# Building the turned one-hots of graph attention on ScalarE instead of VectorE

## The chip, the cores and the metric

The kernel is one program on one core of a Trainium2 chip. The metric is the device time of one execution in microseconds (us), taken as the median of several runs. TensorE is called PE in the profile, VectorE DVE, ScalarE ACT, GpSimd POOL and SyncE SP.

## The reference, cut to what matters

Four graph layers run over 6250 nodes (7 tiles of 128 rows at a time, 49 tiles in all) and 206,250 edges that are sorted by destination. The change lies in the third of the four, a graph attention with three inner layers and four heads:

```python
def _gat_layer(x, src, dst, W_i, a_src_i, a_dst_i, b_i):
    h = (x @ W_i).reshape(n, H, C)
    es = einsum('nhc,hc->nh', h, a_src_i)
    ed = einsum('nhc,hc->nh', h, a_dst_i)
    e = es[src] + ed[dst]                       # a score for each edge and head
    e = where(e > 0, e, 0.2 * e)
    m = segment_max(e, dst); p = exp(e - m[dst])
    denom = segment_sum(p, dst)
    out = segment_sum((p / denom[dst])[:, :, None] * h[src], dst)
```

The lookup `ed[dst]` is done as a matrix product: for 128 edges at a time a matrix with nodes on partitions and edges along the row, one where the node is the edge's destination and zero elsewhere, is multiplied with the nodes' scores. That matrix is the "turned one-hot", `pick_t`. The plain one-hot `pick` (edges on partitions) sums the weighted rows by destination.

## The kernel before, in words

The edges are cut into slots of 128, and 32 slots make a group. An attention layer has 52 groups, so the three layers have 156. Each group goes through these steps, and neighbouring groups overlap:

- **Gather (POOL, L649).** 32 indirect DMAs, one for each slot, fetch the rows of the source nodes from `row_table` into one of two halves of `gathered`. Before each round of 8 POOL waits for `att.summed`: the sums of the group that used this half two groups earlier. POOL does nothing else in an attention layer. In all there are 4992 of these gathers.
- **Destination scores.** SP loads the destinations of the group's edges, the same for all partitions, into `pick_t` (L508, 128 x 4096 bf16, 1 MB). Two instructions (L1769, `build_pick_t`) turn this in place into one-hots by comparing each number with the partition's own index. PE multiplies them with `dst_parts` (L1110, `score_some`).
- **Scores, maxima, exponents (DVE with PE and ACT).** `score_edges` waits for the landing of the whole group's gathers and ends in L1782 and L1785; `first_scans` (L1792, L1794), `carries` (L1799 to L1807), `last_scans` (L1813 to L1824) and `shift_scores` (L1829 to L1834) find the maximum of each destination. ACT takes the exponents (L829, L831).
- **Weighing and summing.** For each batch of 4 slots DVE weighs the gathered rows (`weigh`, L1853), PE multiplies them with `pick` (`sum_batch`, L1182), and DVE adds the results to `acc` (`add_batch`, L1866).
- **Plain one-hots (ACT).** `act_picks` builds 8 slots of `pick`: 8 instructions at L804 (the distance between a column's number and the edge's destination) and one at L807 (one less the distance, cut at zero).

The order is written out by hand in `dve_group`, `pe_group` and `act_group`. While group g is summed in its eight batches m = 0 to 7, the steps of group g+1 are put between the batches on DVE: scores after m = 0, first scans after 1, carries and the first half of `build_pick_t` (for group g+2) after 2, last scans and the second half of `build_pick_t` after 3, the shift after 5. In the first two layers DVE also scans edge attributes after m = 4 and m = 6 (`scan_edges`, L1535 and L1537), whose results PE turns (L1122) and ACT copies (L755).

ACT goes through a group in this order: `stage` (L824: it waits until the next group's gathers have landed and writes the indices of the group after that), then for each quarter q of the group `act_picks`, which waits until PE has summed the batches of that quarter; between the third and the fourth quarter come `scan_out` and `act_exps`.

The semaphores that tie this together: SP counts up `att.rows_loaded` when a load of `pick_t` has landed; who builds counts up `att.turned` once for each half; PE waits for it in `score_some` and counts up `att.dst_scored`, for which SP waits before the next load.

```python
def build_pick_t(part_no):
    ks = slice(part_no * GROUP // 2, (part_no + 1) * GROUP // 2)
    dve.tensor_scalar(pick_t[:, ks, :], pick_t[:, ks, :], part_index[:, 0:1], None,
                      ALU.is_equal).then_inc(att.turned, 1)
```

## Time and profile before

| what | value |
|---|---|
| median of 3 runs | 9245.97 us (9245.64 to 9248.44) |
| the profiled execution's own time | 9241.63 us |
| its span, first to last instruction | 9239.8 us |
| mean granted TensorE clock | 0.642 of full speed |
| PE busy | 5626.5 us, 61% |
| DVE busy | 5638.8 us, 61% |
| ACT busy | 3271.8 us, 35% |
| POOL busy | 5375.1 us, 58% |
| HBM | 106 GB/s over the span |

"Busy" counts the time in which an engine's instructions run, over the whole span; the stages have different limits, so a share says little by itself. In a row of the costliest groups, the numbers behind the first bar are the busy time in us and the mean duration of one instruction in ns, and those behind the second bar are the idle time of the engine before these instructions and what ended most of it. "issue" means that the engine waited for nothing that the profile shows. In a timeline each row has the start in us, the time in us, the engine, the line of the kernel, the operation, what it writes and reads, and how many instructions it merges; in brackets the idle time before it.

### The profile page before, as it was taken

The page shows a single profiled execution, that of the slowest core. Times are in us where ns is not written, and L with a number is a line of the kernel's source. Part 1 is how long each engine was busy: PE and PEld are TensorE (multiplying, and loading weights), DVE is VectorE, ACT ScalarE, POOL GpSimd, SP SyncE. Part 2 cuts the span into 40 slices and gives each one's busy share as a digit, 9 for nine tenths or more (in the row PEclk, how much of TensorE's full clock was granted, in tenths as well). Part 3 has the DMA queues.
Part 4 walks back from the last instruction along what each step waited for, and adds up shares of the span by engine and source line. Part 5 has one row for each costly group of instructions (what it writes and reads, how often), then busy time and mean ns, then how long its engine had stood idle before and what let it go on. Part 6 is the DMA issues. An engine that isn't in the chain of part 4 may idle for free.

```text
span 9239.8 us, 129442 instructions
## 1 busy us (share of the span) xinstructions
PE 5626.5 (61%) x34288; PEld 4513.0 (49%) x34288; DVE 5638.8 (61%) x13019; ACT 3271.8 (35%) x7522; POOL 5375.1 (58%) x5192
## 2 busy tenths in 40 slices
PE   4999879964555555555455555555534545445456
PEld 3777646653544445444444444454434444444444
DVE  6888721135666666666466666666645555555555
ACT  3555400023333333333343333333323333333334
POOL 2000100047777777775677777777657777777770
PEclk9999989965555555555555555555555555555558
DMA  3333335404444444443344444444423333233321
GB/s 101 136 139 139 125 140 192 175 16 120 119 119 116 122 113 124 114 116 82 96 113 118 119 116 121 113 123 113 104 65 80 85 80 85 79 85 80 85 79 32
DMA packets 601474, 989.07 MB, mean 107 GB/s; under 512 B 331107, under 2 KB 455044, under 8 KB 561524
## 3 DMA queue, kind: packets, MB, share of 16 engines
q0 software_dynamic: 163760, 357.05, 17.1%
q1 hardware_dynamic: 217540, 544.34, 16.8%
q10 hardware_dynamic: 219648, 81.82, 3.4%
q8 instruction: 192, 3.15, 0.1%
q14 instruction: 334, 2.73, 0.1%
HBM read 758.42 MB, written 224.34 MB: 106 GB/s over the span
## 4 chain that ended last, share of the span: by engine, by line
PE 27%; DVE 22%; DVEq 18%; POOL 14%; issue 13%; DMA 5%; ACT 1%; POOLq 0%; SPq 0%; ACTq 0%
DVEq L1264 15%; PE bank L959 13%; POOL arena L649 13%; DVE acc L1866 10%; DMA arena<-row_table,staged_idx 4%; PE bank L1182 3%; PE bank L984 3%; DVE arena L1853 2%; DVE arena L1822 2%; PE bank L1122 2%; DVEq L1866 2%; DVE x_mem L1535 1%; DVE arena L1815 1%; DVEq L1858 1%; PE bank L1247 1%
## 5 line engine op out<-in xcount | busy, mean ns | idle before, releaser
L649 POOL DMA_INDIRECT arena<-row_table,staged_idx x4992 | 5087.9, 1019 | 1626.1 <-issue 1467.3
L1182 PE MATMUL bank<-arena 128*128 128x136 f32 x9984 | 2487.9, 429 | 1207.5 <-DVE acc L1866 1045.8
L1182 PEld LDWEIGHTS bank<-arena 128*128 128x128 f32 x9984 | 2195.9, 316 | 1372.1 <-issue 1231.0
L1866 DVE TENSOR_TENSOR acc<-acc,bank 128x136 f32 x4992 | 1476.7, 296 | 1020.7 <-issue 798.1
L804 ACT ACTIVATE pick_dist<-col,dst_local 128x128 bf16<-128x128 f32 x4992 | 1523.3, 388 | 1092.0 <-PE bank L1182 1091.3
L959 PE MATMUL bank<-arena 128*128 128x385 bf16 (+1 forms) x7546 | 1342.6, 327 | 49.5 <-DVE arena L1639 33.0
L597 POOL TENSOR_TENSOR arena<-acc,node_stat 128x896 f32 x14 | 24.5, 1748 | 1721.8 <-POOLq L609 956.3
L959 PEld LDWEIGHTS bank<-arena 128*128 128x128 bf16 x7546 | 711.2, 98 | 476.5 <-DVE arena L1639 33.2
L1138 PE MATMUL bank<-ident,arena 128*32 128x128 f32 x624 | 161.5, 414 | 1206.8 <-DVE arena L1785 1206.8
L1853 DVE TENSOR_TENSOR arena<-arena,prob 128x528 f32<-128x528 f32 x1248 | 841.6, 695 | 0.2
L1782 DVE TENSOR_TENSOR arena<-arena 128x128 f32<-128x128 f32 x156 | 60.8, 390 | 1229.2 <-DMA arena<-row_table,staged_idx 1229.2
L807 ACT ACTIVATE arena<-pick_dist,ones 128x1024 f32<-128x1024 bf16 x624 | 716.4, 1148 | 45.4 <-issue 3.2
L1508 DVE TENSOR_TENSOR arena<-key_line,x_mem 128x1024 bf16<-128x1024 bf16 x1216 | 690.5, 625 | 65.4 <-PE bank L984 51.6
L1138 PEld LDWEIGHTS bank<-ident,arena 128*32 128x32 f32 x624 | 67.0, 129 | 1258.2 <-DVE arena L1785 1238.6
L745 ACT CAST arena<-bank 128x784 bf16<-128x784 f32 x608 | 507.7, 849 | 409.4 <-PE bank L984 409.4
L1110 PE MATMUL bank<-dst_parts,arena 128*128 x4992 | 480.4, 184 | 160.5 <-issue 107.0
L824 ACT CAST staged_idx<-src_of 128x32 int32<-128x32 f32 x153 | 33.3, 218 | 1529.0 <-DMA arena<-row_table,staged_idx 1529.0
L1110 PEld LDWEIGHTS bank<-dst_parts,arena 128*128 128x128 bf16 x4992 | 390.8, 107 | 249.1 <-issue 190.6
L1122 PE MATMUL bank<-ident,x_mem 96*128 96x96 f32 x1664 | 313.4, 369 | 283.9 <-DVE x_mem L1537 283.9
L1122 PEld LDWEIGHTS bank<-ident,x_mem 96*128 96x128 f32 x1664 | 259.0, 223 | 343.1 <-issue 343.1
L755 ACT COPY x_mem<-bank 128x384 f32<-128x384 f32 x416 | 178.9, 482 | 566.7 <-PE bank L1122 552.2
L984 PE MATMUL bank<-arena 128*128 128x98 bf16 x4864 | 321.9, 210 | 0.0
(354 smaller groups left out, 5383.0 us busy)
## 6 DMA issues: line engine op xcount, KB each, us to landing
arena<-dst_rows SPq DMA_DIRECT2D x156, 1024.0 KB
cell_rows<-arena SPq DMA_DIRECT2D x76, 1568.0 KB, 5.2
arena<-cell_rows SPq DMA_DIRECT2D x76, 1568.0 KB, 6.5
arena<-row_table,staged_idx POOLq DMA_INDIRECT x4992
edge_stats<-x_mem ACTq DMA_DIRECT2D x416, 192.0 KB, 3.5
x_mem<-in_edge_attr SPq DMA_DIRECT2D x208, 192.0 KB
x_mem<-segment_flags SPq DMA_DIRECT2D x416, 96.0 KB
arena<-change_rows SPq DMA_DIRECT2D x312, 64.0 KB
```

The source lines that it names most:

```text
L649: pool.indirect_dma_start(gathered[:, at, :], None, table, bass.IndirectOffsetOnAxis(staged_idx[:, at:at + 1], 0)).then_inc(att_gathered[n ...
L804: nc.scalar.activation(pick_dist[:, k, :], col_index[:, :], ACT.Abs, scale=-1.0, bias=dst_local[:, bass.ds(slot + k, 1)])
L807: nc.scalar.activation(pick[:, where:where + ROUND, :], pick_dist[:, :, :], ACT.Relu, scale=-1.0, bias=ones[:, 0:1]).then_inc(att.picked, 1)
L959: mm = pe.matmul(bank[:, 4 + b, 0:width], cell_mem[f][:, j * P:(j + 1) * P], Hp[:, j, 0:width], start=j == 0, stop=j == NT - 1)
L984: mm = pe.matmul(bank[:, at_bank, at_col:at_col + CELLS], hot_src[:, r // PAIR, :, r % PAIR], hot_cell[:, r // PAIR, :, r % PAIR], start=T ...
L1110: mm = pe.matmul(bank[:, 2, k * PARTS * HEADS:(k + 1) * PARTS * HEADS], pick_t[:, k, :], dst_parts[:, bass.ds(at[k % 4], PARTS * HEADS)], ...
L1122: mm = pe.transpose(bank[:, m, c * 2 * EA:(c + 1) * 2 * EA], scanned[:, c * P:(c + 1) * P], ident[0:2 * EA, 0:2 * EA])
L1182: mm = pe.matmul(region(k)[:, 0:ROW], pick[:, k, :], gathered[:, b * GROUP + k, :], start=True, stop=True)
L1264: dve.drain()
L1508: made = dve.tensor_tensor(hot[:, first:first + UNIT // PAIR, :, :], key_line[:, 0:width * PAIR].rearrange("p (c t) -> p c t", t=PAIR).uns ...
L1853: dve.tensor_tensor(batch_rows, batch_rows, prob[:, b, :, m * BATCH:(m + 1) * BATCH].rearrange("p h s -> p s h").unsqueeze(3) .to_broadcas ...
L1866: done = dve.tensor_tensor(row, row, region(m * BATCH + k), ALU.add)
```

## The change

ScalarE builds `pick_t` in place of VectorE. Where VectorE did it in one instruction for each half (16 slots), ScalarE needs two: the distance of each number from the partition's index (Abs with a bias of minus the index, in place, bf16), then one less the distance, cut at zero (Relu with scale -1 and bias 1, in place). A vector `minus_part` is made for it once, before the layers. In `act_group` the two halves stand behind `act_picks` of the first and of the second quarter. At the start of a layer all four halves (of the first two groups) stand behind the layer's first `act_picks` and before the first `stage`. The waits for `att.rows_loaded` move along. VectorE keeps all else in the same order.

```diff
+        minus_part = sb("minus_part", [P, 1])
...
+            def build_pick_t(rows, part_no):
+                ks = slice(part_no * GROUP // 2, (part_no + 1) * GROUP // 2)
+                if part_no == 0:
+                    act.wait_ge(att.rows_loaded, 16 * rows)
+                    act.sem_inc(act_tick, 1)
+                nc.scalar.activation(pick_t[:, ks, :], pick_t[:, ks, :], ACT.Abs, bias=minus_part[:, 0:1])
+                act.drain()
+                nc.scalar.activation(pick_t[:, ks, :], pick_t[:, ks, :], ACT.Relu, scale=-1.0,
+                                     bias=ones[:, 0:1]).then_inc(att.turned, 1)
...
                             act_picks(q * ROUND, it * (2 * GROUP) + (b + 1) * GROUP + q * ROUND)
+                        if ahead and q < 2:
+                            build_pick_t(n * NG + g + 3, q)
...
+                for part_no in range(2):
+                    build_pick_t(n * NG + 1, part_no)
+                for part_no in range(2):
+                    build_pick_t(n * NG + 2, part_no)
                 stage(0, 0, 0)
...
+            dve.tensor_scalar(minus_part[:, :], part_index[:, :], -1.0, None, ALU.mult)
...
-                def build_pick_t(part_no):
-                    ks = slice(part_no * GROUP // 2, (part_no + 1) * GROUP // 2)
-                    dve.tensor_scalar(pick_t[:, ks, :], pick_t[:, ks, :], part_index[:, 0:1], None,
-                                      ALU.is_equal).then_inc(att.turned, 1)
-
...
-                        if ahead and m == 2:
-                            dve.wait_ge(att.rows_loaded, 16 * (n * NG + 3 + b) + it * 32)
-                            build_pick_t(0)
                         if head and m == 3:
                             last_scans(G + 1, 1 - b)
-                        if ahead and m == 3:
-                            build_pick_t(1)
...
-                dve.wait_ge(att.rows_loaded, 16 * (n * NG + 1))
-                for part_no in range(2):
-                    build_pick_t(part_no)
...
-                dve.wait_ge(att.rows_loaded, 16 * (n * NG + 2))
-                for part_no in range(2):
-                    build_pick_t(part_no)
```

How the order on two engines moves, at the places of which the prediction speaks. First DVE in a group of the first layers, before: the end of `last_scans` (L1819 to L1824), the second half of `build_pick_t` (L1769) and the start of the next weighing.

```order
L1819 TENSOR_TENSOR arena<-arena,cross_rows 32x4
L1822 SCALAR_TENSOR_TENSOR arena<-arena 32x512
L1824 SCALAR_TENSOR_TENSOR arena<-arena 32x512
L1769 TENSOR_SCALAR arena<-arena,part_index 128x2048
L1853 TENSOR_TENSOR arena<-arena,prob 128x4x132
L1858 TENSOR_LOAD offsets
```

The same place with the change, where the lines have other numbers (L1835 and L1837 are the two scans, L1866 is the weighing):

```order
L1832 TENSOR_TENSOR arena<-arena,cross_rows 32x4
L1835 SCALAR_TENSOR_TENSOR arena<-arena 32x512
L1837 SCALAR_TENSOR_TENSOR arena<-arena 32x512
L1866 TENSOR_TENSOR arena<-arena,prob 128x4x132
L1871 TENSOR_LOAD offsets
```

The weighing now follows the second scan directly. The other half of `build_pick_t` goes from behind L1807 in the same way. Then ACT from the start of a group on, before: `stage`, and `act_picks` of three quarters.

```order
L824 CAST staged_idx<-src_of 128x32
L804 ACTIVATE pick_dist<-col,dst_local 128x128 x8
L807 ACTIVATE arena<-pick_dist,ones 128x1024
L804 ACTIVATE pick_dist<-col,dst_local 128x128 x8
L807 ACTIVATE arena<-pick_dist,ones 128x1024
L804 ACTIVATE pick_dist<-col,dst_local 128x128 x8
L807 ACTIVATE arena<-pick_dist,ones 128x1024
```

And with the change (L817 is the distance and L819 the cut, 16 slots each):

```order
L835 CAST staged_idx<-src_of 128x32
L805 ACTIVATE pick_dist<-col,dst_local 128x128 x8
L808 ACTIVATE arena<-pick_dist,ones 128x1024
L817 ACTIVATE arena<-arena,minus_part 128x2048
L819 ACTIVATE arena<-arena,ones 128x2048
L805 ACTIVATE pick_dist<-col,dst_local 128x128 x8
L808 ACTIVATE arena<-pick_dist,ones 128x1024
L817 ACTIVATE arena<-arena,minus_part 128x2048
L819 ACTIVATE arena<-arena,ones 128x2048
L805 ACTIVATE pick_dist<-col,dst_local 128x128 x8
L808 ACTIVATE arena<-pick_dist,ones 128x1024
```

Four instructions of 2048 elements came in between the first and the third quarter; nothing else on ACT changed its place.

## Rows read from the trace of the kernel before

**Rows 1.** The page's costliest groups: POOL's gathers.
```profile
L649 POOL DMA_INDIRECT arena<-row_table,staged_idx x4992 | 5087.9, 1019 | 1626.1 <-issue 1467.3
```

**Rows 2.** L649 alone by layer: ns min/median/max, first and last start in us.
```profile
L649 POOL DMA_INDIRECT arena<-row_table,staged_idx x1664: 940/944/2412, 2079.5 to 4298.0; - x185
...
L649 POOL DMA_INDIRECT arena<-row_table,staged_idx x1664: 940/944/2402, 4450.0 to 6669.3; - x185
...
L649 POOL DMA_INDIRECT arena<-row_table,staged_idx x1664: 938/944/2287, 6856.3 to 9024.5; - x185
```

**Rows 3.** POOL's waits from 2100 to 4290: total us, times, longest us.
```profile
POOL arena L649 <- issue: 480.0, 1574, 0.3
```

**Rows 4.** Timeline of one group of the first layer (4085.03 to 4127.39), rows of DVE and POOL.
```profile
4095.05 0.78 DVE L1769 TENSOR_SCALAR arena<-arena,part_index 128x2048 bf16<-128x2048 bf16 x1
4095.61 1.02 POOL L649 DMA_INDIRECT arena<-row_table,staged_idx  x1 [0.30 <-issue]
4095.75 0.69 DVE L1853 TENSOR_TENSOR arena<-arena,prob 128x528 f32<-128x528 f32 x1
...
4099.51 1.21 DVE L1822 TENSOR_TENSOR_SCAN arena<-arena 32x512 f32<-32x512 f32 x1
4100.69 1.01 POOL L649 DMA_INDIRECT arena<-row_table,staged_idx  x1 [0.30 <-PE bank L1182]
...
4101.94 0.72 DVE L1769 TENSOR_SCALAR arena<-arena,part_index 128x2048 bf16<-128x2048 bf16 x1
4102.01 1.46 POOL L649 DMA_INDIRECT arena<-row_table,staged_idx  x1 [0.30 <-issue]
...
4102.58 0.69 DVE L1853 TENSOR_TENSOR arena<-arena,prob 128x528 f32<-128x528 f32 x1
...
4105.05 1.28 DVE L1535 TENSOR_TENSOR_SCAN x_mem<-x_mem 96x512 f32<-96x512 bf16 x1
...
4107.45 0.68 DVE L1853 TENSOR_TENSOR arena<-arena,prob 128x528 f32<-128x528 f32 x1
4107.52 1.42 POOL L649 DMA_INDIRECT arena<-row_table,staged_idx  x1 [0.30 <-issue]
...
4112.27 1.28 DVE L1535 TENSOR_TENSOR_SCAN x_mem<-x_mem 96x512 f32<-96x512 bf16 x1
4113.00 1.30 POOL L649 DMA_INDIRECT arena<-row_table,staged_idx  x1 [0.30 <-issue]
```

**Rows 5.** Timeline of two other groups nearby, rows of DVE and POOL.
```profile
3970.40 1.21 DVE L1822 TENSOR_TENSOR_SCAN arena<-arena 32x512 f32<-32x512 f32 x1
3970.95 1.64 POOL L649 DMA_INDIRECT arena<-row_table,staged_idx  x1 [0.30 <-issue]
...
3972.83 0.72 DVE L1769 TENSOR_SCALAR arena<-arena,part_index 128x2048 bf16<-128x2048 bf16 x1
3972.90 1.47 POOL L649 DMA_INDIRECT arena<-row_table,staged_idx  x1 [0.30 <-issue]
...
4069.91 1.28 DVE L1535 TENSOR_TENSOR_SCAN x_mem<-x_mem 96x512 f32<-96x512 bf16 x1
4070.01 1.93 POOL L649 DMA_INDIRECT arena<-row_table,staged_idx  x1 [0.30 <-issue]
```

**Rows 6.** Timeline of a third group: its two scans at L1535.
```profile
4019.62 1.28 DVE L1535 TENSOR_TENSOR_SCAN x_mem<-x_mem 96x512 f32<-96x512 bf16 x1
...
4027.21 1.28 DVE L1535 TENSOR_TENSOR_SCAN x_mem<-x_mem 96x512 f32<-96x512 bf16 x1
```

**Rows 7.** L1769 alone: duration, first and last start, and what it waited for.
```profile
L1769 DVE TENSOR_SCALAR arena<-arena,part_index x312: 703/734/797, 2097.3 to 9001.4; 128x2048 bf16<-128x2048 bf16 x156
...
  DMA arena<-dst_rows: 6.9, 1
```

**Rows 8.** The page's costliest groups: ACT's plain one-hots.
```profile
L804 ACT ACTIVATE pick_dist<-col,dst_local 128x128 bf16<-128x128 f32 x4992 | 1523.3, 388 | 1092.0 <-PE bank L1182 1091.3
...
L807 ACT ACTIVATE arena<-pick_dist,ones 128x1024 f32<-128x1024 bf16 x624 | 716.4, 1148 | 45.4 <-issue 3.2
```

## Prediction

> **What bounds the kernel now.** I read the page first: PE and DVE are both busy for 61% of the span, ACT for 35%, POOL for 58%, and no share names a bound. So I took the attention layers apart, since the change lies in them alone. The row of POOL's gathers [rows 1] shows 4992 of them with 5087.9 us busy, and an idle time of which nearly all is "issue". By layer [rows 2] they run from 2079.5 to 4298.0, from 4450.0 to 6669.3 and from 6856.3 to 9024.5, which is 6606 us of the 9240. The question is whether POOL waits for anybody inside a layer. It does not: in the first layer its longest wait of 1574 is 0.3 us [rows 3], the pause that follows every gather. The 0.94 us of a median gather and that pause (1.247 us together) make 39.9 us for a group of 32, but a layer of 52 groups takes 42.7 us for each (2219 us) and the last one 41.7 us (2169 us). What is missing lies inside the gathers: 5087.9 less 4992 times 0.944 is 375 us, in gathers that take up to 2.4 us instead of 0.94 [rows 1, 2]. **The layers are bound by POOL's gathers, and only the length of a gather can move their time.** The chain of waits gives DVE a large share, but POOL never stands still for DVE's results.
>
> What makes a gather long is seen in the timeline [rows 4]. The gather at 4107.52 takes 1.42 us; a weighing (L1853) began 0.07 us before it and ended at 4108.13, 0.61 us into it. The gather at 4113.00 takes 1.30 us; the scan L1535 runs until 4113.55. The gather at 4102.01 takes 1.46 us beside a L1769 that began 0.07 us earlier. Each time the gather ends 0.75 to 0.82 us after the DVE instruction does. So a gather that starts while DVE is inside an instruction with its inputs in SBUF is held until that instruction ends, and one that starts first is not: L1822 at 4099.51 began 0.07 us after its gather, which took the plain 1.25 us to the next one at 4100.69. The scan L1822 holds longest: in another group it began 0.55 us before a gather, which took 1.64 us [rows 5]. What a DVE instruction costs is therefore decided by its place against the gathers, to 0.1 us.
>
> The Trainium skill (page "SBUF — State Buffer", section "Who interferes with whom") says that DVE and GpSimd share one pair of ports, that a tensor_scalar in a two-port mode locks GpSimd out, and that a tensor_tensor with both inputs in SBUF does so only against GpSimd's reads, so not against the writing of descriptors. The trace agrees with the lock and not with the exception: gathers are held behind L1853 and L1535 too [rows 4]. By that rule only L1769 would hold gathers, which is the second rival below.
>
> **The change part by part.**
> *ACT gets four instructions of 2048 elements for each group.* L804 takes 388 ns for 128 elements and L807 takes 1148 ns for 1024 [rows 8], 0.85 ns for each further element, so one of 2048 takes about 2.0 us and a group 8.1 us. Before its L804 ACT idles 1092 us for PE's sums, 7.0 us in each of 156 groups, and the builds stand right there. So about 1 us may run over into the third quarter, whose one-hots are wanted a whole group later. Cost 0; if that cover were gone it would be 8.1 us for each group on ACT, which is busy 35%. PE gets the first half of `pick_t` earlier than before. The load of the destinations must have landed a few us earlier than for DVE; DVE waited for it once in 312 times, at the start of the first layer [rows 7], so it landed well ahead. If it did land late, ACT would stand and POOL would not notice, up to the some 8 us that ACT has left. The bounds of this part are 0 and, were all four instructions to delay POOL, 8.1 us times 156; nothing in the rows points above 0.
>
> *Start of a layer.* ACT builds four halves (16 us) behind the first one-hots, while the first group's 32 gathers need 40 us to land. Hidden; 0.
>
> *DVE loses L1769, 312 times.* It frees 0.70 us at the first place (L1769 at 4095.05, the next weighing at 4095.75) and 0.64 us at the second (4101.94 to 4102.58) [rows 4]. As time on DVE this is worth nothing, because POOL does not wait for DVE. But two things follow for the gathers. L1769 no longer holds any; and all of DVE's instructions behind it, in a chain without idle time worth the name, come 0.70 and then 1.34 us earlier against gathers that keep their beat. Walking through the group of [rows 4] with a beat of 1.247 us:
> - Before, from the first L1769 on: holds of 0.08 (4095.61), 0.07 (4100.69), 0.52 (4102.01), 0.48 (4107.52) and 0.36 us (4113.00), together 1.51. One hold behind the last weighings stays as it is.
> - After: at 4095.61 L1853 runs until 4095.74, too short to hold. The third gather behind it starts at 4099.35. L1822 now starts at 4098.81, 0.54 us before: this is the case of 3970.95, 1.64 us [rows 5], a hold of **0.70**.
> - The next starts at 4101.29 or 4101.30. The weighing of 4102.58 stands at 4101.24, where in the odd group L1769 stood (3972.83 against 3972.90, 1.47 us) [rows 5]. By the case of 4107.45, another **0.49**.
> - Two gathers on, 4104.28: L1535 runs from 4103.71 to 4104.99, so the gather ends 0.75 us behind that, a hold of **0.52**.
> - Five on, 4111.03: the second L1535 starts at 4110.93, 0.10 us before. That is the case of 4069.91 and 4070.01, 1.93 us [rows 5], a hold of **0.99**.
> Together 2.70 against 1.51, so such a group gets **1.2 us longer**. The scan L1822 had stood in the lucky place just behind a gather's start, and leaves it.
>
> In some groups the second scan comes 0.35 us later on DVE: 7.59 us behind the first in [rows 6], 7.22 us in [rows 4]. There it meets the end of a gather, the 0.99 becomes about 0.1, and the sum is +0.3 or, with the small terms, near 0. I count two groups in three as the first kind: 2/3 of 1.19 is 0.79 us for each of the 100 groups with a build in the first two layers, 79 us. The last layer has no edge scans, so only L1822 and the weighing behind it count: 0.70 and 0.49 in place of 0.08, 0.07 and 0.52, +0.5; in two of three groups, 0.35 times 50 is 17 us. The sum is +96 us; for the places where 0.05 us decides I take **+90**.
>
> The profiled execution took 9241.6 us (span 9239.8), 4.3 us under the median of the runs. 9241.6 and 90 are 9331.6; with the 4.3 us the median becomes 9336, and I round to 9335.
>
> **The rivals.**
> 1. *The holds fall elsewhere, to both sides of zero.* DVE is delayed a little where a gather comes first, by 0.2 or 0.35 us, and my two closest cases have the DVE instruction only 0.06 and 0.10 us ahead of the gather. If the gather wins both, 1.48 us of the 2.70 go, and a group of the first kind becomes 0.3 us shorter: -30 us over two layers, and at the last layer about 0, so some 9216. If only the closer one goes, +0.7 in the first kind: about 9290. This is also the case against "faster": averaged over all possible places, two scans of 1.2 us in a beat of 1.25 us are seldom out of the way.
> 2. *Faster: only L1769 holds anyone, or its removal moves nobody into a bad place.* Then each group gets back 0.08 and 0.52 us, 0.6 us times 150 = 90 us: 9156. Point of decision: whether L1822 starts before or behind its gather. For it: the largest single hold of the group, 0.52 us, is L1769's. Against it: the holds by L1853 and L1535 in the same rows, and nothing keeps DVE from running on 0.7 us earlier. By the Trainium skill's rule named above this would be the outcome, and the trace does not bear its exception out.
> 3. *No change.* The holds given up and the new ones balance, or POOL's length is set by something else: 9246.
> 4. *Much slower: ACT is late for `stage`,* which writes POOL's next indices behind the landing of a group. It has about 40 us before POOL wants them, and with the builds ACT works 24 of the 42 us of a group (3271.8 us over 156 groups at the most, and 8.1). I see no place for it; 2%.
>
> **How the numbers follow.** My forecast, slower by 50 to 150 us, gets 0.64. Rival 1 between +18 and +50 us, or above my range, gets 0.10, and rival 4 gets 0.02. Within 18.5 us of no change (0.2%, about what a measurement of this kernel can tell) 0.11. Faster, by rival 2 or the full rival 1, 0.13. So slower 0.76, same 0.11, faster 0.13. If every group of the first two layers were of the first kind, +120, and all of the last layer +0.5, +25, the time would be 9391; the lower end takes in the case in which both close gathers win, 9225. That leaves out most of rival 2 and rival 4.
>
> **What would show it.** POOL's pauses stay at 0.3 us and its median gather at 944 ns; the mean of L649 goes from 1019 to about 1037 ns. In a usual group the gather beside L1822 takes about 1.64 us and the one behind it about 1.45. ACT's busy time grows by 624 times 2.0, about 1260 us, and DVE's falls by some 220. If the gather beside L1822 stays at 0.94 us, the walk is wrong at its first step; if POOL shows waits of over 1 us, the bound is another.

## Result and profile after

The changed kernel takes 9205.89 us (median of 5 runs, 9201.93 to 9206.76) against 9245.97 us (9244.49 to 9248.44): ratio 0.9955, 95% interval 0.9945 to 0.9966. It is 40 us **faster**; 9335 (9225 to 9391) had been forecast. The profiled execution took 9206.7 us (span 9204.5), 35 us less than that of before.

The page's costliest groups of after; L650 is the gather (L649 before), L817 and L819 are ACT's new instructions:

```profile
L650 POOL DMA_INDIRECT arena<-row_table,staged_idx x4992 | 5039.4, 1009 | 1624.7 <-issue 1504.0
...
L805 ACT ACTIVATE pick_dist<-col,dst_local 128x128 bf16<-128x128 f32 x4992 | 1518.5, 387 | 59.2 <-PE bank L1199 58.5
...
L817 ACT ACTIVATE arena<-arena,minus_part 128x2048 bf16<-128x2048 bf16 x312 | 624.4, 2001 | 71.6 <-DMA arena<-dst_rows 33.2
L819 ACT ACTIVATE arena<-arena,ones 128x2048 bf16<-128x2048 bf16 x312 | 624.5, 2002 | 22.0 <-issue 0.7
```

ACT's part is as forecast: 2.0 us each, 1249 us in all, most of it taken out of the idle time ahead of the one-hots (1092.0 in [rows 8], now 59.2). The gathers became shorter, 5087.9 to 5039.4 us [rows 1]; 1037 ns had been forecast for their mean, not 1009. POOL still waits for nobody inside a layer, and its median gather is still 944 ns (compare [rows 2, 3]). First POOL's waits from 2100 to 4280, then the gathers alone:

```profile
POOL arena L650 <- issue: 493.7, 1619, 0.3
POOL arena L650 <- PE bank L1199: 7.9, 26, 0.3
```
```profile
L650 POOL DMA_INDIRECT arena<-row_table,staged_idx x4992: 940/944/1935, 2090.0 to 8986.7; - x200
```

So the bound was named rightly, and the gathers' 48.5 us are the gain: the three spans of gathers are 15, 14 and 19 us shorter, 48 in all. The profiled execution shows 35 of it, because its first gather starts at 2090.0 in place of 2079.5 and the last stage takes 2 us more. The 10 us arise ahead of the attention layers, in the second of the four graph layers, where the change adds and moves nothing. The same 322 matmuls take 65 us before and 77 after, at a granted TensorE clock of 0.81 and of 0.63 (start and end in us, length, busy us and instructions of PE, PEld, DVE, ACT and POOL, granted clock, DMA; first the trace of before, then that of after):

```profile
1900.00:1965.00 65.00, 55.85 (x322) 44.21 (x322) 17.55 (x16) 11.00 (x10) 39.60 (x20) 0.81 0.00 0
```
```profile
1899.00:1976.00 77.00, 68.34 (x322) 53.82 (x322) 18.15 (x16) 11.01 (x10) 39.71 (x20) 0.63 0.00 0
```

So PE spent more of this stretch at the lower of its two levels. The profiles of e1 to e4 below have it too, the one with the comparison back at both places included (first gather at 2088.5). Why the clock fell sooner, and whether the change has a part in it, stays open: of the kernel before there is one profile.

What DVE no longer does for `pick_t` it spends largely in waiting for the landing of the gathers: its wait ahead of L1795 (L1782 before) is 1381.7 us, against 1229.2. The two rows, of before and of after, one view each (the instruction alone, its idle time by what ended it: us, times):

```profile
  DMA arena<-row_table,staged_idx: 1229.2, 156
```
```profile
  DMA arena<-row_table,staged_idx: 1381.7, 156
```

The timeline of a usual group of after, rows of DVE and POOL, answers [rows 4] (L1866 is the weighing, L1807 the second of the first scans, L1835 and L1837 the last scans, L1553 and L1555 the edge scans):

```profile
4093.51 0.95 POOL L650 DMA_INDIRECT arena<-row_table,staged_idx  x1 [0.30 <-issue]
...
4096.71 1.21 DVE L1835 TENSOR_TENSOR_SCAN arena<-arena 32x512 f32<-32x512 f32 x1
4097.26 1.42 POOL L650 DMA_INDIRECT arena<-row_table,staged_idx  x1 [0.30 <-issue]
4097.99 1.21 DVE L1837 TENSOR_TENSOR_SCAN arena<-arena 32x512 f32<-32x512 f32 x1
4098.98 0.97 POOL L650 DMA_INDIRECT arena<-row_table,staged_idx  x1 [0.31 <-issue]
4099.13 0.67 DVE L1866 TENSOR_TENSOR arena<-arena,prob 128x528 f32<-128x528 f32 x1
...
4101.51 0.94 POOL L650 DMA_INDIRECT arena<-row_table,staged_idx  x1 [0.30 <-issue]
4101.58 1.28 DVE L1553 TENSOR_TENSOR_SCAN x_mem<-x_mem 96x512 f32<-96x512 bf16 x1
...
4103.96 0.68 DVE L1866 TENSOR_TENSOR arena<-arena,prob 128x528 f32<-128x528 f32 x1
4104.01 1.45 POOL L650 DMA_INDIRECT arena<-row_table,staged_idx  x1 [0.30 <-issue]
...
4108.78 1.28 DVE L1553 TENSOR_TENSOR_SCAN x_mem<-x_mem 96x512 f32<-96x512 bf16 x1
4109.50 1.31 POOL L650 DMA_INDIRECT arena<-row_table,staged_idx  x1 [0.30 <-issue]
```

In this group L1835 starts 0.55 us ahead of the gather at 4097.26, exactly the distance of [rows 5] (3970.40 and 3970.95) and of the walk. But the gather takes 1.42 us, not 1.64: it ends 0.76 us after the scan, where that of before ended 0.98 after it. So the next gathers start 0.22 us sooner than forecast. That of 4098.98 would have met the weighing L1866 with 0.06 us to spare; now it starts 0.15 us ahead of it and takes 0.97. The one beside the first L1553 starts 0.07 us ahead of the scan. What is held then is a weighing (4104.01, 0.50 us) and the end of the second L1553 (4109.50, 0.36). Together 0.48 + 0.03 + 0.50 + 0.36 = 1.37 us, in the place of 2.70 forecast and 1.51 before.

One group is not the kernel. The next table adds up, over all three layers, what gathers took beyond 0.944 us each (those under 0.97 us left out), put down to the DVE instruction during which the gather started:

| DVE instruction | before, us | after, us |
|---|---|---|
| comparison (L1769) | 104.5 | none |
| first last scan (L1822, now L1835) | 32.4 | 80.0 |
| weighing (L1853, now L1866) | 107.1 | 116.7 |
| edge scans (L1535, now L1553) | 51.8 | 53.3 |
| second of the first scans (L1794, now L1807) | 72.6 | 68.8 |
| all others | 8.1 | 9.7 |
| together | 376.5 | 328.5 |

The comparison's holds went, and the first last scan took back nearly half of them: beside it 0.21 us a gather in the mean became 0.52.

### The profile page after: what moved, and what is told of

Read it like the earlier page. It is cut to its first block, busy times and chain, and to the rows that moved or that the text cites. A ratio compares the mean times of both kernels' runs of the same rounds, so it can differ in the third digit from the quotient of the medians.

```text
span 9204.5 us, 130223 instructions
## 1 busy us (share of the span) xinstructions
PE 5638.7 (61%) x34288; PEld 4521.8 (49%) x34288; DVE 5424.6 (59%) x12708; ACT 4487.3 (49%) x8146; POOL 5326.3 (58%) x5192
## 4 chain that ended last, share of the span: by engine, by line
PE 27%; DVE 21%; DVEq 17%; POOL 16%; issue 13%; DMA 5%; ACT 1%; POOLq 0%; SPq 0%; ACTq 0%
POOL arena L650 14%; DVEq L1281 14%; PE bank L976 13%; DVE acc L1879 10%; DMA arena<-row_table,staged_idx 4%; PE bank L1199 3%; PE bank L1001 3%; DVE arena L1835 2%; PE bank L1139 2%; DVEq L1879 2%; DVE arena L1866 2%; DVE x_mem L1553 1%; DVE arena L1828 1%; PE bank L1264 1%; DVEq L1871 1%
## 5 line engine op out<-in xcount | busy, mean ns | idle before, releaser
L650 POOL DMA_INDIRECT arena<-row_table,staged_idx x4992 | 5039.4, 1009 | 1624.7 <-issue 1504.0
L805 ACT ACTIVATE pick_dist<-col,dst_local 128x128 bf16<-128x128 f32 x4992 | 1518.5, 387 | 59.2 <-PE bank L1199 58.5
L1795 DVE TENSOR_TENSOR arena<-arena 128x128 f32<-128x128 f32 x156 | 60.8, 390 | 1381.7 <-DMA arena<-row_table,staged_idx 1381.7
L1866 DVE TENSOR_TENSOR arena<-arena,prob 128x528 f32<-128x528 f32 x1248 | 837.3, 691 | 0.5
L817 ACT ACTIVATE arena<-arena,minus_part 128x2048 bf16<-128x2048 bf16 x312 | 624.4, 2001 | 71.6 <-DMA arena<-dst_rows 33.2
L819 ACT ACTIVATE arena<-arena,ones 128x2048 bf16<-128x2048 bf16 x312 | 624.5, 2002 | 22.0 <-issue 0.7
```

The costliest lines, as they stand in the source:

```text
L650: pool.indirect_dma_start(gathered[:, at, :], None, table, bass.IndirectOffsetOnAxis(staged_idx[:, at:at + 1], 0)).then_inc(att_gathered[n ...
L805: nc.scalar.activation(pick_dist[:, k, :], col_index[:, :], ACT.Abs, scale=-1.0, bias=dst_local[:, bass.ds(slot + k, 1)])
L819: nc.scalar.activation(pick_t[:, ks, :], pick_t[:, ks, :], ACT.Relu, scale=-1.0, bias=ones[:, 0:1]).then_inc(att.turned, 1)
L1866: dve.tensor_tensor(batch_rows, batch_rows, prob[:, b, :, m * BATCH:(m + 1) * BATCH].rearrange("p h s -> p s h").unsqueeze(3) .to_broadcas ...
```

## The experiments

Two things had to be told apart: is it really the place of DVE's instructions that decides (theory of holds), and where do the 0.22 us come from? A useless comparison on unused SBUF, or another useless instruction, is put back at one place or the other on DVE, while ACT keeps the real work. From the traces of before and after I had made a table of holds: a gather that starts over 0.05 us inside a DVE instruction with SBUF inputs ends 0.76 us after it (scan) or 0.82 (weighing, comparison). "Walk" below is that table laid over a trace whose DVE instructions are moved.

**A comparison at one place, at both, or a fill.** The edit on the changed kernel:

```
+        spare_f = x_mem[:, 5056:6080]
+        spare = spare_f.bitcast(BF16)
...
+            dve.memset(spare_f[:, :], 0.0)                      # e2 to e4, once, before the layers' groups
...
                         if head and m == 2:
                             carries(G + 1, 1 - b)
+                        if ahead and m == 2:                    # e2, e4 (e1: dve.memset(spare_f[:, 0:820], 0.0))
+                            dve.tensor_scalar(spare[:, :], spare[:, :], part_index[:, 0:1], None, ALU.is_equal)
                         if head and m == 3:
                             last_scans(G + 1, 1 - b)
+                        if ahead and m == 3:                    # e3, e4 (e1: dve.memset(spare_f[:, 0:745], 0.0))
+                            dve.tensor_scalar(spare[:, :], spare[:, :], part_index[:, 0:1], None, ALU.is_equal)
```

e1, fills at both places: 

> The changed kernel, and on VectorE a memset of 820 and one of 745 numbers of unused memory where the two halves of build_pick_t stood: VectorE keeps the places it had in the kernel before (0.70 and 0.64 us later than in the changed one), without a tensor_scalar. Theory of the holds (POOL's gathers bound the layers, a gather is lengthened by a VectorE instruction with its inputs in SBUF in whose midst it starts, and a tensor_scalar queued behind the two last scans adds 0.22 us to a hold behind the first of them): walking every group of both traces with these rules gives 42.3, 42.3 and 40.9 us for a group of the three layers, against 42.5, 42.5 and 41.35 in the changed kernel, so 40 us less than that: 9166. Rival A (the gain came from VectorE's shorter path): the stand-ins take back all of it, 9246. Rival B (only the tensor_scalar's own holds counted, places do not matter): the same as the changed kernel, 9206.

e2, comparison at the first place: 

> The changed kernel, and on VectorE a tensor_scalar of the shape of build_pick_t, on unused memory, at the first of the two places only (behind the carries). Theory of the holds: 42.5, 42.6 and 41.4 us for a group, 9 us more than the changed kernel: 9215. Rival A: half of the gain goes, 9226. Rival B: the first tensor_scalar's own hold of 0.08 us comes back in each group, 12 us: 9218.

e3, at the second: 

> The same with the tensor_scalar at the second place only (behind the last scans). Theory of the holds: the scan L1835 stays 0.55 us ahead of a gather, its hold gets the further 0.22 us, and the weighing behind falls on the next gather: 43.1, 43.1 and 42.0 us for a group, 99 us more than the changed kernel and slower than the kernel before: 9305. Rival A: half of the gain goes, 9226. Rival B: the second tensor_scalar's own 0.52 us comes back in each group, 78 us: 9284 at most, and under 9246 together with the rest.

e4, at both: 

> The same with the tensor_scalar at both places: VectorE is as before the change, while ScalarE builds the one-hots. All theories of VectorE give the time of the kernel before, 9246. If ScalarE's 8 us for each group or its earlier readiness of pick_t counted for anything, the time would differ from 9246 by just that.

Measured, beside the kernel before at 9240.05 us:

| run | median us | ratio to before, 95% | L652, mean ns |
|---|---|---|---|
| e1 fills | 9567.12 | 1.0351 (1.0334 to 1.0369) | 1082 |
| e2 first | 9154.58 | 0.9904 (0.9888 to 0.9921) | 999 |
| e3 second | 9306.90 | 1.0069 (1.0052 to 1.0086) | 1029 |
| e4 both | 9243.28 | 1.0003 (0.9993 to 1.0012) | 1017 |

e4 is the kernel before in time, though ACT also does its new work: **the move to ACT costs and gains nothing that the time shows**, and the gain of the change comes from what DVE's schedule does to gathers. That the ratio is so near to 1 is in part chance: in the profiled executions e4 starts its first gather 9 us later than before (the clock above), and its gathers take 10 us less (5077.6 us against 5087.9), spread over many lines, in a comparison of one profile with one. Useless work makes the kernel 51 us faster than the changed one at one place (9154.58) and 101 slower at the other (by the ratios 47 and 105, since the changed kernel was not run again beside them): no account by DVE's busy time can give both signs. e3 came out within 2 us of its walk, and its groups take 43.1, 43.1 and 42.1 us, where 43.1, 43.1 and 42.0 had been walked. In its timeline the comparison (L1906) stands two behind the first last scan (L1838) again:

```profile
4082.44 1.21 DVE L1838 TENSOR_TENSOR_SCAN arena<-arena 32x512 f32<-32x512 f32 x1
4082.99 1.64 POOL L652 DMA_INDIRECT arena<-row_table,staged_idx  x1 [0.30 <-issue]
4083.72 1.21 DVE L1840 TENSOR_TENSOR_SCAN arena<-arena 32x512 f32<-32x512 f32 x1
4084.86 0.71 DVE L1906 TENSOR_SCALAR x_mem<-x_mem,part_index 128x2048 bf16<-128x2048 bf16 x1
4084.94 1.46 POOL L652 DMA_INDIRECT arena<-row_table,staged_idx  x1 [0.30 <-issue]
```

The same 0.55 us, and the 1.64 us are back. That is the 0.22. The other traces bear it out, at gathers that started inside the first last scan: with the comparison two behind they end 0.98 us after it (median of 45 in before, 153 in e3, 44 in e4), without it 0.76 us (153 in after, 153 in e1, 41 in e2).

e2 missed (9215 expected). Its mechanism holds in its own trace: in the group shown both last scans and the weighing start level with a gather or just behind it, the lucky place, and none of these gathers is held:

```profile
4081.24 0.94 POOL L652 DMA_INDIRECT arena<-row_table,staged_idx  x1 [0.30 <-issue]
4081.31 1.21 DVE L1838 TENSOR_TENSOR_SCAN arena<-arena 32x512 f32<-32x512 f32 x1
4082.49 0.94 POOL L652 DMA_INDIRECT arena<-row_table,staged_idx  x1 [0.30 <-PE bank L1201]
4082.59 1.21 DVE L1840 TENSOR_TENSOR_SCAN arena<-arena 32x512 f32<-32x512 f32 x1
4083.74 0.94 POOL L652 DMA_INDIRECT arena<-row_table,staged_idx  x1 [0.30 <-issue]
4083.74 0.73 DVE L1869 TENSOR_TENSOR arena<-arena,prob 128x528 f32<-128x528 f32 x1
```

But the walk was too long in every layer: 42.5, 42.6 and 41.4 us a group, where e2's groups take 42.1, 42.1 and 41.1. The last layer has no edge scans, so their place cannot be the whole of it. As an estimate, the table laid over the trace of after with all DVE work behind the first place moved shows how steep the ground is: a shift of 0.70 us gives 42.5, 42.5 and 41.3, a shift of 0.76 us 42.0, 42.0 and 40.9. With the places of e2's own trace the table gives 42.1, 42.1 and 41.0. So the table describes; what it forecasts is only as good as the places put in, to 0.06 us.

e1 missed by far. Its fill was meant as a stand-in that takes DVE's time and holds nobody, and it holds more than the comparison:

```profile
4122.09 1.21 DVE L1839 TENSOR_TENSOR_SCAN arena<-arena 32x512 f32<-32x512 f32 x1
4123.08 2.38 POOL L652 DMA_INDIRECT arena<-row_table,staged_idx  x1 [0.30 <-issue]
4123.41 0.68 DVE L1907 MEMSET x_mem<- 128x745 f32 x1
4124.02 0.63 DVE L1868 TENSOR_TENSOR arena<-arena,prob 128x528 f32<-128x528 f32 x1
```

The gather started inside the scan, and ends 0.81 us after the weighing that is two instructions on: it was handed from one instruction to the next. So do nearly all the gathers that start there, one in each group (0.82 us past the weighing in the median), and another in each group starts inside the other fill and takes 1.75 us: together 217 and 126 us of holds beyond the plain 0.944 us, more than the 313 us by which all gathers of e1 grew.

**Each kind of instruction by itself.** A kernel of its own: POOL issues gathers of the same shape in a loop, DVE repeats one step and a small copy of changing width.

> A kernel of its own that computes nothing of the reference: POOL issues row gathers of the kernel's form without a stop while DVE repeats one step 60 times, with a small copy out of a bank of changing width between, so that a gather starts at every place against the step. Thirteen steps in turn, each on a line of its own. Theory of holds, from the traces so far: a gather that starts over 0.05 us inside a scan with two SBUF inputs ends 0.76 us after the scan, inside a weighing or a comparison (tensor_scalar) 0.82 us after it, inside a fill (memset) likewise; so single gathers up to 1.9 us beside the scan (1.21 us), 1.4 beside the weighing (0.67), 1.5 beside the comparison and the fill. Beside a scan or an add with a bank input, beside a copy out of a bank, and beside ACT's 2.0 us activations on the turned destinations: 0.94 like alone. A copy from SBUF to SBUF: open. Two scans and then a comparison, as in the kernel before, against two scans and then a weighing, as in the changed one: the gather that starts inside the first scan ends 0.98 us after it with the comparison and 0.76 with the weighing, the step of the prediction that failed. Rival (the kind of instruction is not the cause, the holds of the kernel come from its waits and transfers): all steps alike. Rival (each kind has its hold, but the 0.22 us has another cause in the kernel): the two rows of scans are alike.

It settles the 0.22 us outside of the kernel. First the timeline of the scans that a comparison follows (L172, L176, L160), then of those that a weighing follows (L152):

```profile
1451.23 1.21 DVE L172 TENSOR_TENSOR_SCAN seg_f<-flag,grp_sb 32x512 f32<-32x512 f32 x1
1451.77 1.66 POOL L118 DMA_INDIRECT gathered<-row_table,staged_idx  x1 [0.30 <-issue]
1452.52 1.21 DVE L176 TENSOR_TENSOR_SCAN seg_m<-flag,seg_f 32x512 f32<-32x512 f32 x1
1453.66 0.72 DVE L160 TENSOR_SCALAR spare<-spare,part 128x2048 bf16<-128x2048 bf16 x1
1453.73 1.47 POOL L118 DMA_INDIRECT gathered<-row_table,staged_idx  x1 [0.30 <-issue]
...
1800.84 1.21 DVE L172 TENSOR_TENSOR_SCAN seg_f<-flag,grp_sb 32x512 f32<-32x512 f32 x1
1801.41 1.40 POOL L118 DMA_INDIRECT gathered<-row_table,staged_idx  x1 [0.30 <-issue]
1802.12 1.21 DVE L176 TENSOR_TENSOR_SCAN seg_m<-flag,seg_f 32x512 f32<-32x512 f32 x1
1803.12 0.98 POOL L118 DMA_INDIRECT gathered<-row_table,staged_idx  x1 [0.30 <-issue]
```

1451.77 + 1.66 is 0.99 us after the first scan's end (1452.44), 1801.41 + 1.40 is 0.76 after it (1802.05). Counted over the timeline, gathers that started at least 0.06 us inside the step and over 0.16 us before its end:

| step on DVE | started inside | held | end after DVE's end, us |
|---|---|---|---|
| scan, two SBUF inputs | 60 | 60 | 0.76 |
| scan, one input from a bank | 44 | 0 | |
| first of two scans, then a comparison | 59 | 59 | 0.98 (median) |
| first of two scans, then a weighing | 32 | 30 | 0.76 |
| weighing | 37 | 37 | 0.82 |
| add, one input from a bank | 26 | 0 | |
| fill, the small copy behind it | 19 | 0 | |
| copy out of a bank, the small copy behind it | 28 | 0 | |
| copy from SBUF to SBUF | 6 | 6 | 0.82 |
| ACT's Abs of 2048 elements | 87 | 0 | |

Beside the comparison alone all that started over 0.1 us inside it were held, the median ending 0.82 us after it. The small copy out of a bank (a drain stands on either side of it) held nobody ahead of six kinds of steps, but all 25 gathers ahead of a comparison that followed at once (0.95 us after its end). So it is also what is **queued next** on DVE that decides: the fill with a drain and the small copy behind it is harmless, while the fill of e1, with a weighing directly behind it, was not. Not every neighbour counts. A weighing directly behind a comparison left the end at 0.81 us after the comparison (29 held of 35), and directly behind a scan with two SBUF inputs at 0.76 us after the scan (32 of 36).

The Trainium skill (page "SBUF — State Buffer", section "Who interferes with whom") says that two SBUF inputs collide with a GpSimd instruction that reads SBUF, and that an instruction with at most one, outside the two-port modes, does not. I had not asked what a gather reads: its indices lie in SBUF (`staged_idx` in its rows). Read so, the first, second, fifth and sixth rows of this table agree with it. The rival that I had drawn from the exception for a tensor_tensor falls with rows one and five. But the fill of e1, and the copy of e16 and the second scan of e17 below, have at most one SBUF input and gathers were held beside them; there the measurement decides.

**Other useless work, and scans without two SBUF inputs.** On the changed kernel, at the first place, a copy out of a bank of 512 or 256 columns (e5, e6):

```
+                        if ahead and m == 2:
+                            dve.tensor_copy(spare_f[0:GROUP, 0:512], grp[:, 0:512])
```

and the last scans worked in the bank, without (e7) or with (e8) the copy out of it as useless work:

```
                     def last_scans(head, b):
...
-                    dve.tensor_copy(grp_sb, grp)                 # stays in e8
...
-                    dve.tensor_tensor(grp_sb[:, 0::P], grp_sb[:, 0::P], cross_rows[:, 0:HEADS], ALU.max)
+                    dve.tensor_tensor(grp[:, 0::P], grp[:, 0::P], cross_rows[:, 0:HEADS], ALU.max)
...
-                    dve.tensor_tensor_scan(seg_f, start_flag[:, b, :], grp_sb, FAR, ALU.add, ALU.max)
+                    dve.tensor_tensor_scan(grp, start_flag[:, b, :], grp, FAR, ALU.add, ALU.max)
...
-                    dve.tensor_tensor_scan(seg_m[:, ::-1], end_flag[:, b, ::-1], seg_f[:, ::-1], FAR,
+                    dve.tensor_tensor_scan(seg_m[:, ::-1], end_flag[:, b, ::-1], grp[:, ::-1], FAR,
```

> The changed kernel, and at the first of the two places a useless copy of 32x512 out of a PSUM bank into spare SBUF, a form that no trace shows to hold a gather; it takes 0.67 us and moves all DVE work behind it by about 0.70 us. Theory of places (a gather is held only where it starts inside a DVE instruction with two SBUF inputs, so DVE's place against POOL's grid decides): a walk over the changed kernel's own trace with everything behind the place 0.7 us later gives 41.91, 41.94 and 40.80 us a group in place of 42.46, 42.51 and 41.33, which is 85 us less: 9121 us (9105 to 9140), though DVE does 105 us more. Rival operands alone (only the kind of a DVE instruction counts, not where it stands; a copy from a bank is harmless): 9206. Rival DVE's own path: 9206 or more, up to 9206 + 105 = 9311.

> The same with half the copy, 32x256, about 0.40 us, so a shift of about 0.43. Theory of places: the same walk gives 42.72, 42.75 and 41.62, 40 to 50 us more than the changed kernel: 9250 us (9235 to 9265); the cliff to a gain lies at a shift of 0.55 us. So half of the useless work is to cost time where the whole of it gains some. Rival operands alone: 9206. Rival DVE's own path: between 9206 and the time of the full copy, if that is slower.

> The changed kernel, with the two last scans and the two small maxima in front of them working in the PSUM bank itself, so the 0.67 us copy out of it (L1828) goes and neither scan has two SBUF inputs. Theory of places: the holds beside both scans go (0.5 us a group and what stands behind the second), but all DVE work from there on starts 0.7 us sooner and runs into other gathers: the walk gives 42.50, 42.53 and 41.18, 4 us less than the changed kernel: 9202 us; at a shift of only 0.5 it would be 9100, so 9095 to 9210. Rival operands alone: the holds that went are gained whatever happens to places, about 0.5 us x 156 = 75 us: 9130. Rival DVE's own path: 0.7 us x 156 = 109 us gained: 9097.

> The same, but the copy stays as useless work, so that nothing moves. Theory of places: the two scans hold nothing, all else stands: walk 42.22, 42.17, 40.83, 56 us less than the changed kernel: 9150 us (9135 to 9175), and faster than the version without the copy. Rival operands alone: 9130, like the one without the copy. Rival DVE's own path: 9206.

The times of these runs, and of the same kernels taken up again in e9 to e17, could not test the walk: beside them the kernel before took 10322 to 10388 us. POOL's page row of e15 (the full copy) shows an idle time of 2765.4 us, where that of after has 1624.7, at gathers that are no longer:

```profile
L652 POOL DMA_INDIRECT arena<-row_table,staged_idx x4992 | 4985.9, 999 | 2765.4 <-issue 1774.3
```

and e15's waits over the whole execution (us in total, times, longest us):

```profile
POOL arena L652 <- issue: 1774.3, 4722, 9.2
DVE acc L1881 <- remote: 1106.6, 176, 15.2
ACT staged_idx L837 <- DMA arena<-row_table,staged_idx: 1081.0, 144, 15.5
```

DVE stood 1106.6 us ahead of its adds for something that the profile cannot name ("remote"), which no row of after has, and PE's products had ended 4.3 us (median) before such a wait did. POOL's pauses before a gather exceeded 0.4 us 412 times inside the layers, 370 of them ahead of a round of 8, where POOL's wait for the sums stands (median 3.0 us; in after none did). Each such wait starts its beat anew. The expectations of e9 to e17 put this down to gathers landing 4 us late. That was read from DVE's next instruction, which was late itself; by ACT's L837 the landing came 1.65 us after the last gather (median of 144 waits; 4.2 or more in one of ten), against 1.63 in after. So a late landing is only a part, and what made the waits long stays open. It is not the chip alone: one chip gave 9240 us beside e1 to e4 and 10388 beside e5 to e8. Ratios to the kernel before, run on the same chip each time:

| set | before, us | copy 512 | copy 256 | scans in bank, no copy | scans in bank, copy |
|---|---|---|---|---|---|
| e5 to e8 | 10388.04 | 0.9983 (0.9970 to 0.9996) | 1.0000 (0.9988 to 1.0013) | 0.9904 (0.9887 to 0.9920) | 0.9944 (0.9927 to 0.9961) |
| e9, e10 | 10321.62 | 1.0004 (0.9988 to 1.0019) | 0.9998 (0.9984 to 1.0012) | | |
| e11 to e14 | 10341.30 | 0.9964 (0.9945 to 0.9984) | 0.9993 (0.9977 to 1.0009) | 0.9947 (0.9931 to 0.9964) | 0.9953 (0.9937 to 0.9968) |
| e15 to e17 | 10371.07 | 0.9957 (0.9941 to 0.9974) | 1.0018 (1.0007 to 1.0029) | | 0.9955 (0.9936 to 0.9974) |

What was expected of the last three of them, with the reason for taking these kernels up again:

> The useless 32x512 copy out of a bank at the first place, once more, for a grid of POOL's that no late landing breaks. Theory of places: 9121 us (9105 to 9140), ratio 0.9865. Rival operands alone 9206 (0.9955); rival DVE's own path 9206 to 9311.

> The useless 32x256 copy at the same place. Theory of places: 9250 us (9235 to 9265), ratio about 1.0005. Rival operands alone 9206 (0.9955).

> The last scans work in the bank, with the copy kept as useless work. Theory of places: 9150 us (9135 to 9175), ratio 0.990. Rival operands alone 9130; rival DVE's own path 9206.

None of the expected times came. In three of four sets the larger useless copy is the faster one, clearly so only in the last (intervals apart), which is the walk's sign but not its size, and not a proof. For the scans in the bank the walk had the useless copy make the kernel faster (9150 against 9202); in the first set it made it slower (0.9944 against 0.9904, intervals apart), which is the sign of the rival DVE's own path, and in the other set that has both they are alike. On a beat that waits for the sums DVE's own path can count, so this decides nothing for the undisturbed one. What these traces can show is the single gather. e17, a gather 0.55 us inside the first last scan, whose input now lies in the bank:

```profile
4104.89 1.22 DVE L1835 TENSOR_TENSOR_SCAN bank<-arena,bank 32x512 f32<-32x512 f32 x1
4105.44 0.94 POOL L650 DMA_INDIRECT arena<-row_table,staged_idx  x1 [0.30 <-issue]
```

It takes 0.94 us, against 1.42 in after at the same distance. All 127 such gathers of e17 take 0.94 or 0.95 us, the 153 of after 1.47 on average. So the inputs decide there, as in the kernel of its own. But the second scan of e17, which also has one input in the bank, stands directly ahead of the weighing, and it does hold:

```profile
5437.64 1.21 DVE L1837 TENSOR_TENSOR_SCAN arena<-arena,bank 32x512 f32<-32x512 f32 x1
5437.79 1.40 POOL L650 DMA_INDIRECT arena<-row_table,staged_idx  x1 [0.30 <-issue]
5438.78 0.67 DVE L1866 TENSOR_TENSOR arena<-arena,prob 128x528 f32<-128x528 f32 x1
```

Of 116 gathers that started inside it 92 took longer than 0.96 us, and they end 0.35 us after the scan (median), where a scan with two SBUF inputs holds them to 0.76. And e16 shows that my stand-in was again no neutral one:

```profile
3043.39 0.41 DVE L1903 COPY x_mem<-bank 32x256 f32<-32x256 f32 x1
3043.47 1.76 POOL L652 DMA_INDIRECT arena<-row_table,staged_idx  x1 [2.59 <-remote]
3043.72 0.69 DVE L1868 TENSOR_TENSOR arena<-arena,prob 128x528 f32<-128x528 f32 x1
```

The gather started inside a copy out of a bank and is held to 0.82 us past the end of the weighing queued directly behind it, as are all 24 of e16 to within 0.01 us. In e15 all 30 that started inside the full copy were held, most of them to 0.75 us after the copy. The copy L1828, which reads the same bank but is followed by a drain, held none of 134 in after. The walks for e5 and e6 left this out, so they would have been off even on an undisturbed beat.

## Why the prediction was wrong

- **What bounds the layers** was right: POOL waits for nobody (0.3 us at most), the median gather is 944 ns, and only the lengths of gathers moved. e2 and e3, faster and slower by the same useless work, confirm it.
- **ACT's part, cost 0,** was right as far as the time can tell: e4 has the ratio 1.0003 (0.9993 to 1.0012) with the new work on ACT and the old time still spent on DVE, though 9 us of clock and 10 us of gathers cancel in its profile.
- **DVE's shift** of 0.70 and 1.34 us was right: L1835 stands 0.55 us ahead of its gather, 0.54 had been forecast; the weighing starts 0.15 us behind its gather, which is 0.07 ahead of it once the 0.22 is added back, and 0.06 had been forecast.
- **The step that failed is the hold beside L1822, "the case of 3970.95, 1.64 us, a hold of 0.70".** It measured 0.48. I had taken a duration from a row of before in which the comparison still stood two instructions behind the scan, and that comparison is what the change removes. It was part of the cause: e3 brings it back and has 1.64; the kernel of its own has 0.98 against 0.76 us after the scan with only the instruction behind the two scans changed.
- **From there on the chain went wrong by itself.** The 0.22 us moved every later gather. The 0.49 rested on 0.06 us and became 0.03, the 0.52 fell away, the 0.99 became 0.36 and a weighing held one for 0.50: -0.14 us in the group shown where +1.19 had been forecast. Over all groups the mean is -0.31 us; by layer the span shrank by 15, 14 and 19 us. Is the one term enough for all of it? No run changes it alone. As an estimate, the table of holds laid over the places of after gives 42.3, 42.3 and 41.4 us a group (measured 42.5, 42.5 and 41.4), and with 0.22 us more beside L1835 and nothing else 43.4, 43.4 and 42.0. That is some 150 us for the three layers, and the forecast of +90 missed the measured -48 by 138.
- **Rival 1** had named this: the holds fall elsewhere, and the margins of 0.06 and 0.10 us are where it turns. It shared a chance of 0.13 with rival 2 and stopped at 9216. That it came within 10 us is in part luck: it had the gather win for another reason (DVE late), kept the 0.70, and could not know of the 10 us of clock ahead of the layers. **Rival 2** (only L1769 holds) is dead: without it 5039.4 less 4992 times 0.944 is still 327 us of holds. The range was too narrow for a sum of four terms, two of which hung on 0.06 and 0.10 us; its lower end should have held all four at their other value.

Open: why the clock fell sooner ahead of the layers; why an instruction queued behind lengthens a hold; and whether the walk forecasts a place it has not seen. One that it forecast came (e3), one did not (e2), and four kernels met a broken beat.

## What to carry to other kernels

When an engine that never waits is the bound, and its instructions are held up by a neighbour's, taking work off the neighbour is worth nothing in itself; it re-deals the places, and the sign of the result is decided by tenths of a microsecond. Price a collision only from rows in which the instructions *behind* it are also those of the changed kernel, give each near miss both values in the range, and expect useless stand-ins to collide too. Operands remove such holds only together with a harmless neighbour: a scan with one input in a bank and a drain behind it held none of 127 gathers, the next one, with a weighing directly behind it, 92 of 116. And try the useless instruction: here e2, with 0.7 us of nothing in each group, beats both kernels, 0.9904 (0.9888 to 0.9921) against 0.9955 (0.9945 to 0.9966).

## What the runs showed of the hardware that I had not expected

- The hold of a gather depends on DVE's queue, not only on the instruction it meets: 0.98 in place of 0.76 us after a scan when a comparison is two behind, with a second scan between.
- A fill, a copy out of a bank or a scan with one bank input held nobody with a drain behind it (0 of 19, of 28, of 44 in m1; the copy only if no comparison followed). With a weighing directly behind, gathers were held: to 0.82 us after the weighing beside fill and copy (1.75 us in e1, 1.76 in e16; also the 2.38 us of e1, which began in the scan ahead of the fill), to 0.35 us after the scan in e17. Why the three differ stays open.
- The kernel before took 9240 us beside e1 to e4 and beside m1 and 10322 to 10388 beside e5 to e17; two of the chips gave both. Gathers and scans took as long as ever (a plain gather 0.94 us, a scan 1.21); waits between engines ended late, mostly with no releaser in the profile.
